# Graph attention and mean aggregation on one core: 45 far chunks with 8 walk blocks each in place of 55 with 6, found rows sent off by ScalarE, smaller opening products, four table buffers

## The chip, the core and the metric

The kernel runs on one core of one Trainium2 chip. A core has five engines that run their own instruction streams in order and wait for one another by semaphores: TensorE (PE, with its weight loads PEld), VectorE (DVE), ScalarE (ACT), GpSimd (POOL) and SyncE (SP). SyncE only issues DMA transfers here; ScalarE and GpSimd issue some too. The metric is the device time of one execution in microseconds (us), and the kernels are compared by the median over runs.

## The reference

There are N = 12,500 nodes with 64 features and E = 400,000 edges sorted by destination; each edge has one of 32 relation types. A first layer computes attention over the incoming edges of each node, a second takes a mean over neighbours:

```python
h_proj = jnp.einsum('nd,rde->rne', h, relation_weight)
t_r = h_proj[etype, src]
h_r = h_proj[etype, dst]
att = jnp.sum(t_r * jnp.tanh(h_r + efeat), axis=-1)
att_exp = jnp.exp(att - segment_max(att, dst)[dst])
a = att_exp / segment_sum(att_exp, dst)[dst]
h_nb = segment_sum(h[src] * a[:, None], dst)
out = leaky_relu((h + h_nb) @ res_w1.T) + leaky_relu(h * h_nb @ res_w2.T)
# x = layernorm(x + out); then x = layernorm(x + mean over in-neighbours of x / out_degree)
```

## The kernel before

The program first writes a table in HBM: for every pair (relation, node) the projected row (64 numbers), together with the node's own row. That is the table stage. Then it goes through the edges in 125 chunks, each of 25 edges on each of 128 partitions. Every edge needs two rows of the table: one for its source (`gs`) and one for its destination (`gd`). After that come short stages for the nodes, for the second layer and for the output, which the diff does not touch.

The source rows are fetched by GpSimd with indirect DMAs, 25 per chunk (L1542). For the destination rows there are two ways, and a chunk is far or near by which it uses.

- In a **far chunk** (the first `FAR` = 55) GpSimd fetches the destination rows too: 25 more indirect DMAs (L1546), 50 in all.
- In a **near chunk** (the other 70) the destination rows lie ready in a scratch tensor `proj_d` in HBM and come with one plain DMA (L1506).

`proj_d` is filled during the far chunks. Since the edges are sorted by destination, the destination rows of the near chunks lie close together in the table, and a "walk" over windows of the table finds them. The walk has `BLOCKS = PER * FAR` blocks of `K` = 15 steps each, `PER` = 6 blocks within each far chunk. A block works as follows:

- SyncE loads the step keys (`keyb`, L1474, 4 slots `KSLOTS`) and 15 windows of the table (`win`, L1470, `WSLOTS` = 3 slots); the first window's number comes out of `sp_tab` by a register load.
- VectorE compares keys with the lane number and writes a 0/1 matrix (`pick`, L1598, `WSLOTS` slots).
- TensorE reads 16 numbers of the block out of `pe_tab` into registers (L1839), opens two accumulation banks with two products of zeros (L1845, 512 columns each), multiplies 15 times `pick` by a window (L1850, at places that the registers give), and adds one carried row (L1852, L1855).
- ScalarE copies the banks to `found` (L1756, two slots) and SyncE sends them to `proj_d` (L1485).

Within a far chunk the code fixes the places of the blocks in each engine's stream: VectorE makes the `pick` of block 0 and 1 ahead of its wait for the chunk's gathered rows (in `front`), of block 2 behind the first sum (L1619), and of 3 to 5 between the steps of the chunk's attention (`back`). ScalarE has its copies (`take_found`) at six places of `chunk`. TensorE does 25 products for a histogram (L1834, it needs the chunk's one-hot matrices `hi`/`lo` of VectorE, L1585) and then the six blocks. A slot of `win` or `pick` is taken again when the block `WSLOTS` back is done (`found_mm`); block b's zeros wait until ScalarE has copied block b-2. GpSimd may start on a chunk when VectorE has written its indices two chunks earlier (`slot_ready`). The near chunks start when all of `proj_d` is written (`found_out`). L1619 in a far chunk and L1624 in a near chunk are the sum of destination row and edge features, the first step of a chunk's attention.

Of the kernel before, what the change touches and what calls it, by code (L numbers as in the profile page):

```python
# [34 lines left out]
FAR = 55  # L35
# [5 lines left out]
PER = 6  # L41
BLOCKS = PER * FAR
UC = -(-(BLOCKS * K + 1) // P)
KSLOTS, WSLOTS = 4, 3
# [789 lines left out]
def gnn_program(nc, x, src, dst, edge_attr, etype, rel_w, res_w1, res_w2, out):  # L834

    ctx = ExitStack()
    with ctx:
# [547 lines left out]
        with ExitStack() as c2:  # L1385
# [22 lines left out]
            rowbuf = sb(c2, "rowbuf", [P, 2, G, RW])  # L1408
# [4 lines left out]
            after = sb(c2, "after", [P, P])  # L1413
            wide = sb(c2, "wide", [P, 2, P])
            group = sb(c2, "group", [P, P])
            work = sb(c2, "work", [P, P])
            steps = sb(c2, "steps", [P, 2, P])
# [4 lines left out]
            pick = sb(c2, "pick", [P, WSLOTS, K * MT])  # L1422
            found = sb(c2, "found", [P, 2, (K + 1) * D])
# [23 lines left out]
            sp_past = sem(c2, "sp_past")  # L1447
# [9 lines left out]
            with nc.Block() as block:  # L1457
                @block.sync
                def _(sp):
# [17 lines left out]
                    def outputs(b, k):  # L1477
                        i0 = nc.values_load(sp_tab[0:1, bass.ds(2 * b + 1, 1)], engines=[mybir.EngineType.SP],
                                            min_val=0, max_val=TILES - 1, skip_runtime_bounds_check_because=MADE)
                        sp.wait_ge(found_ready, b + 1)  # L1480
                        sp.sem_inc(sp_past, 1)
                        if later(b):
                            sp.wait_ge(found_out, 16 * b)
                        sp.sem_inc(sp_past, 1)
                        sp.dma_start(proj_d[:, bass.ds(i0, K + 1), :],  # L1485
                                     found[:, k, :].rearrange("p (i d) -> p i d", d=D)).then_inc(found_out, 16)
# [29 lines left out]
                    outputs(BLOCKS - 2, 0)  # L1516
                    outputs(BLOCKS - 1, 1)
# [43 lines left out]
                def _(dve):  # L1561
# [39 lines left out]
                    def front(c, s, i, link, far=False):  # L1601
# [7 lines left out]
                        if far:  # L1609
                            picks(c, s, i, 1)  # L1610

                    def back(c, s, i, link, far=False, t0=0, t1=G, before=G):
# [12 lines left out]
                        if far:  # L1625
                            picks(c, s, i, 2)
# [10 lines left out]
                        if far:  # L1637
                            picks(c, s, i, 3)
# [14 lines left out]
                        if far:  # L1653
                            picks(c, s, i, 4)
# [5 lines left out]
                            weight[:, t0:t1].unsqueeze(2).to_broadcast([P, n, D]), ALU.mult))  # L1660
                        for w0, w1 in ((0, WH), (WH, W)):
# [8 lines left out]
                        if far:  # L1670
                            picks(c, s, i, 5)
# [79 lines left out]
                def _(act):  # L1751
                    def take_found(b, k):
                        act.wait_ge(found_mm, b + 1)
                        if later(b) and later(b - 1):
                            act.wait_ge(found_out, 16 * (b - 1))
                        nc.scalar.copy(found[:, k, :], acc[k]).then_inc(found_ready, 1)  # L1756

# [5 lines left out]
                    def chunk(c, s, i, far=False, t0=0, t1=G, follows=None):  # L1763
# [3 lines left out]
                        if far:  # L1767
                            if later(c):
                                take_found(PER * c - 1, 1)
                            take_found(PER * c, 0)  # L1770
                        if t0:
# [8 lines left out]
                        if far:  # L1780
                            take_found(PER * c + 1, 1)
# [8 lines left out]
                        if far:  # L1790
                            take_found(PER * c + 2, 0)
# [3 lines left out]
                        if later(i):  # L1795
                            act.wait_ge(stored[s], 16 * i)
                        nc.scalar.copy(rowbuf[:, s, t0:t1, 0:W], run_t[:, :, 1:].rearrange("p w t -> p t w"))  # L1797
                        nc.scalar.copy(rowbuf[:, s, t0:t1, W], mx[:, 1 + t0:1 + t1]).then_inc(rows_ready, 1)
                        act.wait_ge(rows_ready, k + 1)
                        act.dma_start(sums0_v[:, bass.ds(c * G + t0, n), :], rowbuf[:, s, t0:t1, :]).then_inc(stored[s], 16)  # L1800
                        if far:
                            take_found(PER * c + 3, 1)
                            take_found(PER * c + 4, 0)
# [7 lines left out]
                    take_found(BLOCKS - 1, 1)  # L1811
# [14 lines left out]
                def _(pe):  # L1826
# [10 lines left out]
                    def walk(c, j):  # L1837
# [6 lines left out]
                        for h in range(2):  # L1844
                            nc.tensor.matmul(acc[k][:, h * BANK:(h + 1) * BANK], zero[:, 0:P], zero[:, :], start=True, stop=False)  # L1845
# [11 lines left out]

                    histogram(0)
# [52 lines left out]
```

## Time and profile before

| | |
|---|---|
| median of 3 runs | 8621.35 us (8617.23 to 8623.51) |
| the profiled execution | 8620.08 us, of it 8617.3 us from first to last instruction |
| busy: TensorE products, weight loads | 59%, 54% |
| busy: VectorE, ScalarE, GpSimd | 72%, 38%, 67% |
| DMA | 1142.51 MB, 133 GB/s over the span |

The profile is one execution. "Busy" counts the time in which an engine works on an instruction; register loads and DMA issues on TensorE's, SyncE's and ScalarE's sequencers are not counted. A stage has its own limit, so the shares are to be read by stage: the table stage lasts to 452 us, the far chunks about from there to 4014 us, a handover to 4067 us, the near chunks to 6225 us, and the rest to the end.

### The profile page before, as it was taken

What the parts mean: (1) busy time and instruction counts of PE and PEld (TensorE: products, weight loads), DVE (VectorE), ACT (ScalarE), POOL (GpSimd) and SP (SyncE); (2) the same over time, 40 slices, a digit from 0 to 9 for tenths busy, and PEclk for the clock granted to TensorE, in tenths of its full rate; (3) what the DMA queues carried; (4) which work ended last, traced back from release to release, by engine and by line L of the source; (5) the groups of instructions that cost most, each with busy time, mean ns of one, the idle gap of its engine ahead of it and who ended that gap; (6) DMA issues with size and microseconds to landing.
All of it is one profiled execution on the core that took longest, in us unless ns stands there. A gap on an engine that the chain in (4) does not pass through costs nothing. (4 is left out here: it accounts for less than half of the span.)

```text
span 8617.3 us, 133753 instructions
## 1 busy us (share of the span) xinstructions
PE 5065.6 (59%) x44411; PEld 4657.1 (54%) x44577; DVE 6245.6 (72%) x5544; ACT 3266.4 (38%) x4027; POOL 5800.4 (67%) x5165
## 2 busy tenths in 40 slices
PE   6657777777777777776000000000058999999995
PEld 2247676666676667675000000000048888888885
DVE  4546556556555655656887777777779999999996
ACT  3312222212222212212222222222247888888883
POOL 3767777777777777777777777777644555555544
PEclk8855555555555555555555555555559999999996
DMA  9978878877877878787544444444320000000001
GB/s 391 381 176 183 183 178 181 183 177 180 184 178 177 185 176 179 181 180 174 139 129 132 127 133 133 133 133 133 108 52 10 11 10 10 11 10 10 10 11 32
DMA packets 1216482, 1142.51 MB, mean 133 GB/s; under 512 B 993596, under 2 KB 1047422, under 8 KB 1203200
## 3 DMA queue, kind: packets, MB, share of 16 engines
q1 hardware_dynamic: 1036607, 754.44, 34.5%
q0 software_dynamic: 160592, 281.30, 15.0%
q10 hardware_dynamic: 19200, 105.87, 3.1%
q8 instruction: 26, 0.43, 0.0%
q14 instruction: 57, 0.47, 0.0%
HBM read 697.83 MB, written 444.96 MB: 133 GB/s over the span
## 5 line engine op out<-in xcount | busy, mean ns | idle before, releaser
L1542 POOL DMA_INDIRECT gs<-table,idx_s x3125 | 3009.3, 963 | 980.9 <-issue 965.1
L1850 PEld LDWEIGHTS banks<-win,pick 128*125 128x125 f32 x9900 | 2151.1, 332 | 343.9 <-issue 318.3
L1850 PE MATMUL banks<-win,pick 128*125 (+1 forms) x9900 | 2121.0, 413 | 193.2 <-DVE pick L1598 191.7
L764 ACT CAST columns<-ps_u 128x784 bf16<-128x784 f32 x1968 | 1577.3, 812 | 385.7 <-PE ps_u L794 326.7
L647 POOL DMA_INDIRECT tile_row<-tile_rows,now x123 | 1010.5, 8216 | 977.5 <-PE ps_k L784 922.5
L1546 POOL DMA_INDIRECT gd<-table,idx_d x1375 | 1363.0, 991 | 419.1 <-issue 419.1
L1834 PE MATMUL banks<-hi,lo 128*128 128x98 bf16 x3125 | 279.1, 283 | 2002.4 <-DVE hi L1585 2002.4
L1834 PEld LDWEIGHTS banks<-hi,lo 128*128 128x128 bf16 x3125 | 264.1, 146 | 2017.2 <-DVE hi L1585 2017.2
L802 PE MATMUL ps_s<-parts,columns 128*128 128x192 bf16 x12054 | 1314.8, 248 | 0.4 <-ACT columns L764 0.4
L1619 DVE TENSOR_TENSOR gd<-gd,ef 128x1600 f32<-128x1600 f32 x55 | 100.5, 1827 | 1504.1 <-DMA gd<-table,idx_d 1504.1
L794 PE MATMUL ps_u<-yf,hot_l 125*128 125x98 bf16 x15744 | 1054.1, 210 | 159.5 <-DVE yf L711 155.3
L711 DVE TENSOR_TENSOR hot_l<-iota_two,keys_t 125x8192 bf16<-125x8192 bf16 x246 | 1086.9, 4418 | 0.2 <-PE ps_u L794 0.2
L802 PEld LDWEIGHTS ps_s<-parts,columns 128*128 128x128 bf16 x12054 | 1054.0, 140 | 0.6 <-ACT columns L764 0.6
L794 PEld LDWEIGHTS ps_u<-yf,hot_l 125*128 125x128 bf16 x15744 | 878.6, 98 | 222.6 <-DVE yf L711 190.9
L1756 ACT COPY found<-banks 128x1024 f32<-128x1024 f32 x330 | 332.7, 1008 | 1454.6 <-PE banks L1855 1417.0
L711 DVE TENSOR_TENSOR yf<-iota_two,keys_t 125x6272 bf16<-125x6272 bf16 x246 | 840.7, 3417 | 0.0
L1845 PE MATMUL banks<-zero 128*128 128x512 bf16 x495 | 274.6, 624 | 777.4 <-issue 776.5
L1797 ACT COPY rowbuf<-run 128x1625 f32<-128x1625 f32 (+1 forms) x126 | 411.9, 3269 | 778.6 <-DVE run L1662 778.6
L1598 DVE TENSOR_TENSOR pick<-keyb,banks 128x1875 f32<-128x1875 uint8 x330 | 694.5, 2105 | 14.2 <-DMA keyb<-step_keys 1.0
L1777 ACT COPY prod<-gs 128x1600 f32<-128x1600 f32 (+1 forms) x126 | 190.8, 1514 | 976.9 <-DMA gs<-table,idx_s 975.1
L1662 DVE TENSOR_TENSOR_SCAN run<-banks,add 128x858 f32<-128x858 f32 (+1 forms) x252 | 465.9, 1891 | 4.3
L1845 PEld LDWEIGHTS banks<-zero 128*128 128x128 bf16 x660 | 43.2, 110 | 773.4 <-issue 773.4
(313 smaller groups left out, 5922.7 us busy)
## 6 DMA issues: line engine op xcount, KB each, us to landing
proj_d<-found SPq DMA_DIRECT2D x330, 512.0 KB
win<-table SPq DMA_DIRECT2D x660, 240.0 KB
table<-rows SPq DMA_DIRECT2D x98, 1536.0 KB, 8.9
sums<-rowbuf ACTq DMA_DIRECT2D x124, 825.0 KB
ef<-in_edge_attr_dram SPq DMA_DIRECT2D x125, 800.0 KB, 4.7
keyb<-step_keys SPq DMA_DIRECT2D x332, 234.4 KB, 5.3
gd<-proj_d SPq DMA_DIRECT2D x70, 800.0 KB, 6.0
gs<-table,idx_s POOLq DMA_INDIRECT x3125, 2.6
```

The costliest lines, as they stand in the source:

```text
L647: pool.indirect_dma_start(out=rows[:, j % 2, :], out_offset=None, in_=tile_rows, in_offset=bass.IndirectOffsetOnAxis(ap=now[:, j:j + 1], a ...
L711: hot = nc.vector.tensor_tensor(to[0:MT, b, :, :, :], iota_two[0:MT, first:first + wide, :].unsqueeze(1).to_broadcast([MT, QU // 2, wide, 2]),
L764: nc.scalar.copy(columns[:, j % 2, i * UU:(i + 1) * UU, :].rearrange("p (b u) h -> p b (u h)", b=UB), ps_u[n % 2][:, :, 0:UU // UB * NB]). ...
L794: last = nc.tensor.matmul(ps_u[i % 2][:, t // (UU // UB), t % (UU // UB) * NB:(t % (UU // UB) + 1) * NB], hot_l[0:MT, b, u // 2, :, u % 2] ...
L802: last = nc.tensor.matmul(ps_s[s][:, 0:3 * D], columns[:, s, :, h], parts[:, h, :, :].rearrange("p a d -> p (a d)"), start=h == 0, stop=h ...
L1542: pool.indirect_dma_start(out=gs[:, s, g, :], out_offset=None, in_=table_vec, in_offset=bass.IndirectOffsetOnAxis(ap=idx_s[:, s, g:g + 1], ...
L1546: pool.indirect_dma_start(out=gd[:, s, g, :], out_offset=None, in_=table_vec, in_offset=bass.IndirectOffsetOnAxis(ap=idx_d[:, s, g:g + 1], ...
L1598: nc.vector.tensor_tensor(pick[:, k, :], keyb[:, at % KSLOTS, :], lane_ps.to_broadcast([P, K * MT]), ALU.is_equal).then_inc(pick_ready, 1)
L1662: last = nc.vector.tensor_tensor_scan(run_t[:, w0:w1, :].rearrange("p w t -> p (w t)"), keep[:, 0:(w1 - w0) * (1 + n)], add_t[:, w0:w1, :] ...
L1797: nc.scalar.copy(rowbuf[:, s, t0:t1, 0:W], run_t[:, :, 1:].rearrange("p w t -> p t w"))
L1834: last = nc.tensor.matmul(hist, lo[:, g, :], hi[:, g, :], start=False, stop=False)
L1850: nc.tensor.matmul(acc[k][0:MT, bass.ds(slots[t] * D, D)], pick[:, w, t * MT:(t + 1) * MT], win[:, w, bass.ds(at_w, 1), :].rearrange("p o ...
```

## The change

- `FAR` goes from 55 to 45 and `PER` from 6 to 8. There are 80 near chunks and 45 far ones; the number of walk blocks goes from 330 to 360 (the ten chunks more that are near need their destination rows found as well). The lists that the table stage makes grow with it (`UC` from 39 to 43 rows of step keys).
- `WSLOTS` goes from 3 to 4, for `win` and for `pick`. To make room, `rowbuf` has one slot instead of two, and some small tiles of later use lie inside `pick`.
- VectorE makes the `pick` of block 2 ahead of its wait for the gathered rows, and those of 3 to 7 later in the chunk, with one new place ahead of the two scans.
- ScalarE, not SyncE, sends `found` to `proj_d`: `take_found` reads the place from `sp_tab` into a register, copies, waits for the copy and for the previous transfer's landing, and issues the DMA. Two copies of the previous chunk's end move into the chunk itself.
- The two products of zeros of a block have 64 columns instead of 512. Four products of 512 columns clear the banks once at the start.

```diff
-FAR = 55
+FAR = 45
-PER = 6
+PER = 8
-KSLOTS, WSLOTS = 4, 3
+KSLOTS, WSLOTS = 4, 4
...
-            rowbuf = sb(c2, "rowbuf", [P, 2, G, RW])
+            rowbuf = sb(c2, "rowbuf", [P, G, RW])
...
-                            if j >= 2 or later(c):
-                                outputs(PER * c + j - 2, j % 2)
...
                         if far:
                             picks(c, s, i, 1)
+                            picks(c, s, i, 2)
...
+                        if far:
+                            picks(c, s, i, 6)
                         for w0, w1 in ((0, WH), (WH, W)):
...
                     def take_found(b, k):
+                        i0 = nc.values_load(sp_tab[0:1, bass.ds(2 * b + 1, 1)], engines=[mybir.EngineType.Activation],
+                                            min_val=0, max_val=TILES - 1, skip_runtime_bounds_check_because=MADE)
                         act.wait_ge(found_mm, b + 1)
                         if later(b) and later(b - 1):
                             act.wait_ge(found_out, 16 * (b - 1))
                         nc.scalar.copy(found[:, k, :], acc[k]).then_inc(found_ready, 1)
+                        act.wait_ge(found_ready, b + 1)
+                        act.sem_inc(act_past, 1)
+                        if later(b):
+                            act.wait_ge(found_out, 16 * b)
+                            act.sem_inc(act_past, 1)
+                        act.dma_start(proj_d[:, bass.ds(i0, K + 1), :],
+                                      found[:, k, :].rearrange("p (i d) -> p i d", d=D)).then_inc(found_out, 16)
...
                         for h in range(2):
-                            nc.tensor.matmul(acc[k][:, h * BANK:(h + 1) * BANK], zero[:, 0:P], zero[:, :], start=True, stop=False)
+                            nc.tensor.matmul(acc[k][:, h * BANK:h * BANK + D], zero[:, 0:P], zero[:, 0:D], start=True, stop=False)
```

On ScalarE, in the far chunks' loop, the stretch from the tanh (L1779, after the change L1773) to the copy of the scans' result. Before:

```order
L1779 ACTIVATE gd<-gd 128x1600
L1753 REGISTER_ALU
L1755 REGISTER_ALU
L1756 COPY found<-banks 128x1024
L1783 ACTIVATE banks<-ex_in 128x25
L1784 ACTIVATE decay<-ex_in 128x25
L1788 COPY banks<-decay 128x33x25
L1753 REGISTER_ALU
L1755 REGISTER_ALU
L1756 COPY found<-banks 128x1024
L1796 REGISTER_ALU
L1797 COPY rowbuf<-run 128x25x65
```

and after the change, from the same tanh to the end of the second block's sending:

```order
L1773 ACTIVATE gd<-gd 128x1600
L1738 ISA
L1738 TENSOR_LOAD sp_tab
L1740 REGISTER_ALU
L1743 COPY found<-banks 128x1024
L1747 REGISTER_ALU
L1749 ISA
L1749 DMA proj_d<-found 128x1024
L1777 ACTIVATE banks<-ex_in 128x25
L1778 ACTIVATE decay<-ex_in 128x25
L1782 COPY banks<-decay 128x33x25
L1738 ISA
```

Each copy is now followed by its DMA issue on the same engine, ahead of the exponentials of the attention.

On VectorE, in the same loop, from the chunk's first `pick` to the second one behind it. Before:

```order
L1598 TENSOR_TENSOR pick<-keyb,banks 128x1875
L1617 ISA
L1618 REGISTER_ALU
L1619 TENSOR_TENSOR gd<-gd,ef 128x1600
L1598 TENSOR_TENSOR pick<-keyb,banks 128x1875
```

and after the change (L1580 is the `pick`, L1602 the sum):

```order
L1580 TENSOR_TENSOR pick<-keyb,banks 128x1875
L1579 REGISTER_ALU
L1580 TENSOR_TENSOR pick<-keyb,banks 128x1875
L1600 ISA
L1601 REGISTER_ALU
L1602 TENSOR_TENSOR gd<-gd,ef 128x1600
L1580 TENSOR_TENSOR pick<-keyb,banks 128x1875
```

One `pick` more stands ahead of the sum that waits for the gathered rows, so three blocks can run during that wait instead of two.

## Rows read from the trace of the kernel before

**Rows 1.** Windows: us; busy of PE, PEld, DVE, ACT, POOL; clock, DMA, GB/s.

```profile
0.00:452.00 452.00, 275.59 (x932) 101.45 (x933) 228.93 (x387) 163.48 (x393) 226.20 (x345) 0.82 0.98 384
...
516.00:4014.00 3498.00, 2578.54 (x12527) 2434.70 (x12690) 2000.68 (x1891) 734.63 (x703) 2674.49 (x2703) 0.50 0.80 180
...
4067.00:6225.00 2158.00, 154.66 (x1730) 139.75 (x1730) 1720.76 (x1897) 619.70 (x557) 1609.17 (x1706) 0.50 0.48 131
```

**Rows 2.** Groups, 2000 to 4000 us: busy, mean ns | idle before.

```profile
L1546 POOL DMA_INDIRECT gd<-table,idx_d x771 | 768.0, 996 | 235.0 <-issue 235.0
L1542 POOL DMA_INDIRECT gs<-table,idx_s x772 | 762.9, 988 | 235.3 <-issue 235.3
L1598 DVE TENSOR_TENSOR pick<-keyb,banks 128x1875 f32<-128x1875 uint8 x186 | 391.5, 2105 | 7.7
```

**Rows 3.** Groups of instructions, near stage, 4400 to 6000 us.

```profile
L1542 POOL DMA_INDIRECT gs<-table,idx_s x1283 | 1210.6, 944 | 391.0 <-issue 390.1 <-DVE idx_s L911 0.9
```

**Rows 4.** The line L1619 by source, whole run.

```profile
L1619 DVE TENSOR_TENSOR gd<-gd,ef x55: 1824/1825/1883, 516.0 to 4013.6; 128x1600 f32<-128x1600 f32 x55
```

**Rows 5.** TensorE weight loads, 1785 to 1864 us: start, length, [idle before].

```profile
1800.59 0.13 PEld L1845 LDWEIGHTS banks<-zero 128*128 128x128 bf16 x2 [0.73 <-issue]
...
1808.86 0.13 PEld L1845 LDWEIGHTS banks<-zero 128*128 128x128 bf16 x2 [0.69 <-issue]
1813.67 6.38 PEld L1850 LDWEIGHTS banks<-win,pick 128*125 128x125 f32 x30 [4.68 <-issue]
...
1821.74 0.13 PEld L1845 LDWEIGHTS banks<-zero 128*128 128x128 bf16 x2 [1.16 <-issue]
...
1844.79 0.13 PEld L1845 LDWEIGHTS banks<-zero 128*128 128x128 bf16 x2 [5.48 <-issue]
...
1858.04 0.13 PEld L1845 LDWEIGHTS banks<-zero 128*128 128x128 bf16 x2 [3.66 <-issue]
```

**Rows 6.** Timeline of TensorE's products, same stretch.

```profile
1807.69 0.67 PE L1855 MATMUL banks<-found,ident 128*128 x2
...
1813.67 6.56 PE L1850 MATMUL banks<-win,pick 128*125 128x64 f32 x30 [3.78 <-DVE pick L1598]
```

**Rows 7.** The table load L1839 by source: whole run, then three stretches.

```profile
L1839 PEldq TENSOR_LOAD <-pe_tab x330: 3783/3944/7333, 459.4 to 4042.4; - x165
...
L1839 PEldq TENSOR_LOAD <-pe_tab x2: 3791/3799/3807, 1796.8 to 1805.0; - x2
...
L1839 PEldq TENSOR_LOAD <-pe_tab x1: 5808/5808/5808, 1838.9 to 1838.9; - x1
...
L1839 PEldq TENSOR_LOAD <-pe_tab x1: 4832/4832/4832, 1853.1 to 1853.1; - x1
```

**Rows 8.** Timeline of SyncE's DMA issues, 1838.5 to 1846 us.

```profile
1839.04 0.36 SPq L1485 DMA_DIRECT2D proj_d<-found  x1
...
1844.46 0.62 SPq L1485 DMA_DIRECT2D proj_d<-found  x1
```

**Rows 9.** Timeline of VectorE, 1800 to 1870 us.

```profile
1813.44 0.19 DVE L1633 COPY add<-run 128x33 f32<-128x33 f32 x1
...
1824.14 0.18 DVE L1652 TENSOR_TENSOR ex_in<-ex_in,mx 128x25 f32<-128x25 f32 x1
...
1840.21 2.70 DVE L1585 TENSOR_TENSOR hi<-banks,digit 128x2450 bf16<-128x2450 f32 x1
```

**Rows 10.** Timeline of all engines, 4053 to 4070 us.

```profile
4056.82 1.01 ACT L1756 COPY found<-banks 128x1024 f32<-128x1024 f32 x1 [12.36 <-PE banks L1855]
...
4067.11 1.83 DVE L1624 TENSOR_TENSOR banks<-banks,gd 128x1600 f32<-128x1600 f32 x1 [20.14 <-DMA gd<-proj_d]
```

**Rows 11.** DMA issues of the page: KB each, us to landing.

```profile
proj_d<-found SPq DMA_DIRECT2D x330, 512.0 KB
win<-table SPq DMA_DIRECT2D x660, 240.0 KB
...
keyb<-step_keys SPq DMA_DIRECT2D x332, 234.4 KB, 5.3
```

More of the change, by code:

```diff
@@ L1412, in gnn_program @@
             zero = sb(c2, "zero", [P, BANK], BF16)
[L1413 to L1417, printed above, removed]
             goes_on = sb(c2, "goes_on", [P, 1])
@@ L1422, in gnn_program @@
             pick = sb(c2, "pick", [P, WSLOTS, K * MT])
+            after, group, work = (pick[:, 0, at * P:(at + 1) * P] for at in range(3))
+            wide, steps = (pick[:, 0, at * P:(at + 2) * P].rearrange("p (k j) -> p k j", k=2) for at in (3, 5))
             found = sb(c2, "found", [P, 2, (K + 1) * D])
@@ L1637, in back @@
                         if far:
-                            picks(c, s, i, 3)
+                            picks(c, s, i, 4)
                         dve.wait_ge(tanh_done, k + 1)
@@ L1653, in back @@
                         if far:
-                            picks(c, s, i, 4)
+                            picks(c, s, i, 5)
                         dve.wait_ge(keep_ready, k + 1)
@@ L1670, in back @@
                         if far:
-                            picks(c, s, i, 5)
+                            picks(c, s, i, 7)
                         if go_on:
@@ L1767, in chunk @@
                         if far:
-                            if later(c):
-                                take_found(PER * c - 1, 1)
                             take_found(PER * c, 0)
+                            take_found(PER * c + 1, 1)
                         if t0:
@@ L1780, in chunk @@
                         if far:
-                            take_found(PER * c + 1, 1)
+                            take_found(PER * c + 2, 0)
                         act.wait_ge(exp_arg, k + 1)
@@ L1790, in chunk @@
                         if far:
-                            take_found(PER * c + 2, 0)
+                            take_found(PER * c + 3, 1)
+                            take_found(PER * c + 4, 0)
                         if follows:
@@ L1794, in chunk @@
                         act.wait_ge(run_ready, k + 1)
[L1795 to L1798, printed above, removed]
+                        if s or later(i):
+                            act.wait_ge(stored[1 - s], 16 * (i + s))
+                        nc.scalar.copy(rowbuf[:, t0:t1, 0:W], run_t[:, :, 1:].rearrange("p w t -> p t w"))
+                        nc.scalar.copy(rowbuf[:, t0:t1, W], mx[:, 1 + t0:1 + t1]).then_inc(rows_ready, 1)
                         act.wait_ge(rows_ready, k + 1)
-                        act.dma_start(sums0_v[:, bass.ds(c * G + t0, n), :], rowbuf[:, s, t0:t1, :]).then_inc(stored[s], 16)
+                        act.dma_start(sums0_v[:, bass.ds(c * G + t0, n), :], rowbuf[:, t0:t1, :]).then_inc(stored[s], 16)
                         if far:
-                            take_found(PER * c + 3, 1)
-                            take_found(PER * c + 4, 0)
+                            take_found(PER * c + 5, 1)
+                            take_found(PER * c + 6, 0)
+                            take_found(PER * c + 7, 1)
                     chunk(0, 0, 0, True)
@@ L1856, in walk @@
                                          start=False, stop=True).then_inc(found_mm, 1)
+                    for k in range(2):
+                        for h in range(2):
+                            nc.tensor.matmul(acc[k][:, h * BANK:(h + 1) * BANK], zero[:, 0:P], zero[:, :], start=True, stop=True)
                     histogram(0)
```

17 lines of the change are left out of this document (2 added, 15 removed).

## Prediction, made before the changed kernel was run

> **What bounds the kernel now.** I read the windows by stage first [rows 1]. In the far stage (516 to 4014 us) GpSimd is busy 2674 of 3498 us, TensorE's products 2579, VectorE 2001, ScalarE 735; DMA moves 180 GB/s at a share of 0.80. No engine reads as full, so the share alone decides nothing. The groups of a stretch inside it do [rows 2]: GpSimd's two kinds of gather are busy 768.0 + 762.9 us and idle 235.0 + 235.3 us, together 2001 of 2000 us, and all of that idle time is "issue": it waits for no one. So GpSimd paces the far stage, and 54 chunks from the first L1619 to the last [rows 4] give (4013.6 - 516.0)/54 = 64.8 us for one. In the near stage the same holds [rows 3]: 1210.6 + 391.0 = 1602 us, nearly all issue, 1283 gathers in 1600 us, so 31.2 us for 25.
>
> Then the runner-up of the far stage, TensorE. Its timeline shows blocks that run back to back [rows 5]: the zeros of one block start at 1800.59, those of the next at 1808.86, a pitch of 8.27 us, and the idle time between them (0.69, 0.73) is "issue" again. What fills the pitch is not the array. The register load of the next block starts at 1796.8 and lasts 3.79 us [rows 7]: it ends at 1800.6, where the zeros start. A block is 3.79 us of load and some 4.48 us of issuing, one after the other on TensorE's sequencer, and the array waits for it. The load is never under 3.78 us, with a median of 3.94 and up to 7.33 [rows 7]. Six such blocks and the histogram fit into 64.8 us with room, because the blocks then wait for a `pick` (3.78 us before 1813.67, [rows 6]) or for the step before.
>
> **The gathers (POOL).** Each chunk that turns from far to near saves 25 gathers: 64.8 - 31.2 = 33.6 us, ten chunks 336 us, if GpSimd still paces both stages. That is the gross gain.
>
> **The eight blocks (TensorE).** From block 0 to block 7 there are seven pitches, 7 x 8.27 = 57.9 us. From the chunk's last block to the next chunk's first the histogram comes in between: 1844.79 to 1858.04 [rows 5], 13.25 us. The loads in those 13.25 us last 4.83 us [rows 7], 1.04 over the free ones. The sum so far is 71.1 us for a chunk, over GpSimd's 64.8. **TensorE's sequencer becomes the bound of the far stage.**
>
> **The small zeros.** Two products of 512 columns stand for some 0.8 us of array time. In a back-to-back block they cover nothing that is on the path: the sequencer sets the pitch with or without them, so I take 0 of 0.8 us there. Only ahead of the histogram, whose 25 products must get into the array's queue before the sequencer goes on to its load, does a block that ends earlier help; I take 0.35 us per chunk (bounds 0 and 0.8). If the queue were no limit at all they would be worth nothing anywhere.
>
> **ScalarE sends the rows.** Each block adds to ScalarE a register load, which I bound by one sixteenth of TensorE's, 0.24 us, from below and by 3.8 us from above (a single register speaks for the low end), and a DMA issue of 0.36 to 0.62 us [rows 8]; two copies of 1.0 us [rows 10] are added to each chunk. Its busy time of 21% leaves room. What matters is its order. TensorE's load for block b+1 begins once the copy of block b-1 is made, so a copy may come 5 us late. With the eight blocks back to back and time counted from block 0's zeros, products end at 7.4 + 8.27 j. Block 1 ends at 15.7; its copy, its issue and the copy of the source rows let VectorE go on at about 19. In today's trace L1633 starts at 1813.44 and the one-hots are done at 1842.91 [rows 9], 29.5 us; with one more `pick` of 2.1 us [rows 2] that gives 51, where TensorE's histogram is due at 62. ScalarE's exponentials wait for L1652, 10.9 us behind L1633 [rows 9], so they are due at about 30, ahead of block 3's copy at 32. So I cost this edit at nothing; its cover is some 4 us on ScalarE and 11 us on VectorE, and if it went, each us late would be a us per chunk. It also moves the output issues in time, which matters next.
>
> **What stretches a load.** The load of 5.81 us at 1838.9 has an output issue at 1839.04 and a second at 1844.46 beside it [rows 7, 8]; the one of 4.83 stands at a chunk's end; those of 3.79 have none. I read some 1.0 us for each output issue that falls into a load. After the change ScalarE issues block b's output about 1.4 us behind its last product, just behind the load's end, except at the histogram, where the load comes later; that one stretch is in the 71.1 already. Bounds: none stretched gives 1.0 us less per chunk; as many as in the trace now (one at the histogram, about one in the block before and two in the last) 3.2 us more.
>
> The Trainium skill ("Runtime: NRT & Kernel Launch", Instruction fetch mechanics) puts a register load at about 200 ns for each register, which would make the load of 16 numbers 3.2 us by estimate and the chunk 4.7 us shorter, about 66.1 us; the row says 3.79, 237 ns each, and the measurement decides. By that rule the sum below would come out near 8347 us.
>
> **Windows, keys, DMA.** A block moves 512.0 + 2 x 240.0 + 234.4 KB [rows 11] = 1.23 MB, two more per chunk 2.45 MB on top of 180 GB/s x 64.8 us = 11.7 MB. At a pitch of 70.8 us that is a share of 0.80 x 14.1/11.7 x 64.8/70.8 = 0.88, below the 0.98 that the table stage holds [rows 1]. With four slots a window is asked for three blocks ahead. I cost it at 0; were the share at its end (0.98), the chunk would be 64 us, still under TensorE's. The single `rowbuf` waits for a transfer issued a chunk before: 0. The table stage gets 4 key gathers more among its other work; some 1 us each at most if nothing hides them by the duration of [rows 3], I take 3 us.
>
> **The sum.** Pitch P = 57.9 + 13.25 - 0.35 = 70.8 us. In chunk 0 TensorE waits for the `pick` of block 3: 516.0 + 1.8 + 2.1 = 519.9. Block 4's zeros come 8.07 us later (1821.74 - 1813.67, [rows 5]), block 7's at 552.8. Forty-four pitches on: 552.8 + 3115.2 = 3668.0. Its last product ends 7.8 us behind the zeros (1808.36 - 1800.59, [rows 5, 6]), 7.4 with small zeros: 3675.4. From there to the first near chunk it takes 4067.11 - 4056.82 = 10.3 us [rows 10]: 3685.7, against 4067.1 now, 381.4 us earlier. Ten near chunks more cost 312 us. GpSimd's start into the near stage is as now (two chunks ahead, then it waits for VectorE). Net -69 us, with the table stage -66; against the profiled 8620.1 this is 8554, and the median of the runs shown is 1.3 us above that execution, so **about 8554 us**. Each us of P is worth 44 us, and the change breaks even at P = 72.3.
>
> **The rivals.**
> - *GpSimd still paces the far stage* (TensorE's pitch doesn't add up as I say, for instance since loads overlap issuing when nothing else waits). Against it: the two blocks back to back, where nothing was waited for. It gives 8620 - 336 + 3 = 8287 us. Chance 0.08.
> - *The stretched loads decide, and it gets slower.* ScalarE's output issues or SyncE's fall into the loads of TensorE, 1.0 us each. Break-even is at 1.5 such stretches per chunk beyond the one counted; with three, P = 73.8 and 8686 us; with all eight loads hit, P = 77.8 and 8862. For it: the median load of 3.94 us lies above the free 3.79 [rows 7], so about half are hit now, and an issue of ScalarE comes only some 0.5 us behind a load's end. Chance 0.22.
> - *The array's clock rises.* It is at 0.50 (1.2 GHz) in the whole far stage [rows 1] though products cover 74% of it. At 2.4 GHz a block's pitch would stay, being the sequencer's, but the 13.25 us at the histogram would lose the wait for the queue, about 2.2 us: P = 68.6, 8457 us. The Trainium skill ("TensorE: Matmul & The Clock Gate", What's actually happening) has a busy array go to 2.4 GHz; the far stage's row speaks against it so far. Chance 0.05.
> - Anything else that ties up VectorE or ScalarE inside the chunk: 0.04.
>
> **The numbers.** The forecast has 0.61. Its own range is 8510 (no load stretched) to 8625. Half of the slower rival's weight lies below 8690, the clock's about at 8460, so the range of 8 in 10 is 8455 to 8690. A difference of under 0.2% (17 us) can't be told from none with this kernel; that band is P from 71.9 to 72.7. Faster: most of the forecast and the two fast rivals, 0.68; same 0.10; slower 0.22.
>
> **What the changed profile would show.** GpSimd idle for VectorE's indices in the far stage, some 6 us per chunk, in place of issue only; VectorE's long wait no longer for the gathered rows but for ScalarE's copy of the source rows; block pitches of 8.27 throughout and 12.9 at the histogram, with loads of 3.79 and one of 4.8 per chunk; the first L1624 near 3686; clock 0.50. Wrong: a far chunk of 65 us, pitches above 8.3 with loads of 4.8 and more, or TensorE waiting for a `pick`, a window or a copy.

## The result, and the profile after

| | before | changed |
|---|---|---|
| median | 8622.43 us (8617.23 to 8624.12, 4 runs) | 8684.35 us (8679.44 to 8689.97, 4 runs) |
| ratio, 95% interval | | 1.0076 [1.0064, 1.0087] |
| profiled execution, its span | 8620.08, 8617.3 us | 8687.49, 8685.7 us |

The changed kernel is 62 us slower. It was forecast 66 us faster, at 8554. The rival with stretched loads gave 8686 us for a chunk of P = 73.8 us; the result lies inside the wide range of 8455 to 8690 only since that range held part of this rival.

First the stages. Windows of the changed kernel, columns as in [rows 1]:

```profile
0.00:452.00 452.00, 273.73 (x933) 100.80 (x934) 230.70 (x381) 163.39 (x394) 234.82 (x349) 0.84 0.99 385
520.00:3732.00 3212.00, 2638.52 (x13257) 2535.50 (x13257) 1812.13 (x1628) 686.58 (x656) 2155.53 (x2213) 0.50 0.75 193
```

GpSimd, busy 76% of the far stage before [rows 1], is now busy 67% of it. Its groups and the waits from 2000 to 3500 us (waits: engine, line, what was waited for; us in total, times, longest) say why; they answer to [rows 2]:

```profile
L1528 POOL DMA_INDIRECT gd<-table,idx_d x507 | 508.4, 1003 | 154.5 <-issue 154.5
L1524 POOL DMA_INDIRECT gs<-table,idx_s x508 | 479.4, 944 | 358.7 <-DVE idx_d L916 210.3 <-issue 148.4
...
ACT found L1743 <- PE banks L1850: 1030.7, 163, 13.2
DVE add L1616 <- ACT prod L1771: 466.5, 20, 23.5
PEld banks L1840 <- issue: 289.5, 163, 4.9
PE banks L1840 <- issue: 259.4, 163, 4.7
POOL gs L1524 <- DVE idx_d L916: 210.3, 21, 10.0
```

Once per chunk GpSimd now waits 10.0 us for VectorE's indices; VectorE waits 23.5 us for ScalarE's copy of the source rows, and ScalarE waits for TensorE's blocks (L1850 is a block's last product). TensorE waits for nobody: in front of its zeros (L1840) stands "issue", its own sequencer. That is the chain of waits that the prediction named, with TensorE's sequencer at its head. In its length it differs. Three lines by source give the positions of the chunks (count; min/median/max ns; first and last start): the far sum L1602, the first near sum L1607, and the histogram's products L1829 in the stretch from 600 to 3800 us.

```profile
L1602 DVE TENSOR_TENSOR gd<-gd,ef x45: 1817/1818/1847, 519.8 to 3732.6; 128x1600 f32<-128x1600 f32 x45
...
L1607 DVE TENSOR_TENSOR banks<-banks,gd x81: 743/1833/1833, 3822.5 to 6292.7; 128x1600 f32<-128x1600 f32 x79, 128x1024 f32<-128x1024 f32 x1, 128x576 f32<-128x576 f32 x1
...
L1829 PE MATMUL banks<-hi,lo x1075: 204/285/288, 642.3 to 3740.5; 128*128 128x98 bf16 x180
```

The 1075 products are 43 histograms of 25, and the last product of one starts 2.1 us behind the first, so 42 chunks take 3740.5 - 642.3 - 2.1 = 3096.1 us: **73.7 us per chunk**, where 70.8 was forecast and GpSimd needed 64.8 before. The near stage starts at 3822.5 instead of 3685.7.

One chunk shows where the 2.9 us lie. TensorE's weight loads of the zeros and of the histogram, to be read as [rows 5]; they are the zeros of blocks 3 to 7, the histogram, and block 0 of the next chunk:

```profile
2447.31 0.13 PEld L1840 LDWEIGHTS banks<-zero 128*128 128x128 bf16 x2 [1.12 <-issue]
...
2455.57 0.13 PEld L1840 LDWEIGHTS banks<-zero 128*128 128x128 bf16 x2 [1.13 <-issue]
...
2463.84 0.13 PEld L1840 LDWEIGHTS banks<-zero 128*128 128x128 bf16 x2 [1.03 <-issue]
...
2473.77 0.13 PEld L1840 LDWEIGHTS banks<-zero 128*128 128x128 bf16 x2 [2.79 <-issue]
...
2482.03 0.13 PEld L1840 LDWEIGHTS banks<-zero 128*128 128x128 bf16 x2 [1.13 <-issue]
...
2488.94 2.24 PEld L1829 LDWEIGHTS banks<-hi,lo 128*128 128x128 bf16 x25
...
2495.86 0.13 PEld L1840 LDWEIGHTS banks<-zero 128*128 128x128 bf16 x2 [4.68 <-issue]
```

The pitches are 8.26, 8.27, **9.93**, 8.26 and, over the histogram, 13.83 us. The table load behind each (L1834, now the line of the load) and what the other engines issued meanwhile:

```profile
L1834 PEldq TENSOR_LOAD <-pe_tab x1: 3788/3788/3788, 2460.0 to 2460.0; - x1
...
L1834 PEldq TENSOR_LOAD <-pe_tab x1: 5447/5447/5447, 2468.3 to 2468.3; - x1
...
L1834 PEldq TENSOR_LOAD <-pe_tab x1: 5822/5822/5822, 2489.9 to 2489.9; - x1
```

```profile
2456.06 0.35 ACTq L1749 DMA_DIRECT2D proj_d<-found  x1
...
2464.43 0.35 ACTq L1749 DMA_DIRECT2D proj_d<-found  x1
...
2468.53 0.34 ACTq L1795 DMA_DIRECT2D sums<-rowbuf  x1
...
2472.60 0.34 ACTq L1749 DMA_DIRECT2D proj_d<-found  x1
...
2490.85 0.34 ACTq L1749 DMA_DIRECT2D proj_d<-found  x1
2491.35 0.35 SPq L1458 DMA_DIRECT2D ef<-in_edge_attr_dram  x1
```

Two loads per chunk are long, not one. The load at the histogram (2489.9) has block 7's output issue (L1749) and the issue of the edge features' load (L1458) in it and lasts 5.82 us, 2.03 over the free 3.79; [rows 7] had 4.83 there. The load of block 6 (2468.3), which was forecast free, lasts 5.45 us, 1.66 over. It begins 0.2 us ahead of the issue of the chunk's sums (L1795). A load of 3.79 would have ended at 2472.1, and block 5's output is issued at 2472.60, half a microsecond later; the load, still running, takes that in as well. Elsewhere this load lasts up to 7.02 us (at 1803.2). Over 42 chunks of the trace the load at the histogram has a mean of 5.77 us and block 6's one of 5.89 us (5.37 to 7.02); those of the other six blocks have means of 3.79 to 3.80. An output issued 3.9 us ahead of a load (2456.06, the load at 2460.0) leaves it at 3.79.

### The profile page after: what moved, and what is told of

It reads as the page before. It is cut to its first block and busy times, and to the rows that moved or that the text cites. A ratio compares the mean times of both kernels' runs of the same rounds, so it can differ in the third digit from the quotient of the medians.

```text
span 8685.7 us, 137557 instructions
## 1 busy us (share of the span) xinstructions
PE 5191.0 (60%) x45632; PEld 4820.9 (56%) x45633; DVE 6316.1 (73%) x5554; ACT 3315.2 (38%) x4068; POOL 5513.1 (63%) x4919
## 5 line engine op out<-in xcount | busy, mean ns | idle before, releaser
L1524 POOL DMA_INDIRECT gs<-table,idx_s x3125 | 2966.2, 949 | 1414.9 <-issue 953.1
L1845 PE MATMUL banks<-win,pick 128*125 (+1 forms) x10800 | 2359.9, 418 | 36.6 <-DVE pick L1580 29.5
L1845 PEld LDWEIGHTS banks<-win,pick 128*125 128x125 f32 x10800 | 2294.6, 330 | 76.8 <-issue 50.6
L1829 PE MATMUL banks<-hi,lo 128*128 128x98 bf16 x3125 | 278.6, 283 | 2290.7 <-DVE hi L1567 2290.7
L1829 PEld LDWEIGHTS banks<-hi,lo 128*128 128x128 bf16 x3125 | 261.6, 145 | 2308.5 <-DVE hi L1567 2308.5
L1528 POOL DMA_INDIRECT gd<-table,idx_d x1125 | 1112.8, 989 | 342.8 <-issue 342.8
L1743 ACT COPY found<-banks 128x1024 f32<-128x1024 f32 x360 | 364.3, 1012 | 2310.3 <-PE banks L1850 2310.3
L1580 DVE TENSOR_TENSOR pick<-keyb,banks 128x1875 f32<-128x1875 uint8 x360 | 758.2, 2106 | 367.3 <-PE banks L1850 346.7
L1616 DVE COPY add<-run 128x33 f32<-128x33 f32 x126 | 26.2, 208 | 1338.1 <-ACT prod L1771 1338.1
L1840 PE MATMUL banks<-zero 128*128 128x64 bf16 x720 | 102.3, 236 | 582.4 <-issue 579.1
L1563 DVE TENSOR_TENSOR lo<-banks,digit 128x3200 bf16<-128x3200 f32 x125 | 436.5, 3492 | 4.3
```

The costliest lines, as they stand in the source:

```text
L1524: pool.indirect_dma_start(out=gs[:, s, g, :], out_offset=None, in_=table_vec, in_offset=bass.IndirectOffsetOnAxis(ap=idx_s[:, s, g:g + 1], ...
L1528: pool.indirect_dma_start(out=gd[:, s, g, :], out_offset=None, in_=table_vec, in_offset=bass.IndirectOffsetOnAxis(ap=idx_d[:, s, g:g + 1], ...
L1563: nc.vector.tensor_tensor(lo[:, :, :], iota_ps[:, 0:P].unsqueeze(1).to_broadcast([P, G, P]), digit[:, 0, :].unsqueeze(2).to_broadcast([P, ...
L1580: nc.vector.tensor_tensor(pick[:, k, :], keyb[:, at % KSLOTS, :], lane_ps.to_broadcast([P, K * MT]), ALU.is_equal).then_inc(pick_ready, 1)
L1829: last = nc.tensor.matmul(hist, lo[:, g, :], hi[:, g, :], start=False, stop=False)
L1845: nc.tensor.matmul(acc[k][0:MT, bass.ds(slots[t] * D, D)], pick[:, w, t * MT:(t + 1) * MT], win[:, w, bass.ds(at_w, 1), :].rearrange("p o ...
```

## The experiments

The theory after the result: TensorE's sequencer paces the far stage, and two table loads per chunk are long because ScalarE's transfers fall into them. The rival: another wait or the DMA sets the 73.7 us, which a shorter load would leave in place. Each expectation states what it weighs. Line numbers are those of the kernel that the rows come from. Each group of runs had the kernel before beside it: median 8631.06 us for the first four, 8621.18 for the next four, 8629.93 for the last three.

### What the load costs: four numbers, fourteen numbers

Both leave out a part of the computation: numbers that aren't read are replaced by others of the block, so rows land in wrong places; the products and their sizes are the same.

```diff
-                        _, slots = ...(pe_tab[0:1, bass.ds(16 * b, 16)], ...)
+                        _, four = ...(pe_tab[0:1, bass.ds(16 * b + 12, 4)], ...)
+                        slots = [four[t % 3] for t in range(K)] + [four[3]]
```

(For fourteen: `bass.ds(16 * b + 2, 14)` and `some[t % 13]`.)

> The changed kernel, but TensorE's table load of a block reads 4 numbers instead of 16, and the 15 places of the products repeat the first three of them (so rows land at wrong places; the products, their sizes and the register arithmetic are the same). Theory S (TensorE's sequencer paces the far stage: 4.48 us of issuing plus 3.79 us of load per block, one after the other): the load falls to 4 x 0.237 = 0.95 us, the sequencer needs 5.4 us, the array's 7.4 us per block is next, 8 x 7.5 + 2.5 = 62.5 us is under GpSimd's 64.8, GpSimd paces the far stage again and the kernel takes about 8290 us. Rival W (the blocks wait for picks, windows or ScalarE's copies, and the load only fills a wait): no change, 8670 to 8690 us.

> As the run with four numbers, but 14 of the 16 numbers are loaded (places of two products repeat others). Theory S: 2 x 0.237 = 0.47 us less per block, 3.8 us per chunk, 45 chunks: 8684 - 170 = about 8515 us, block pitch 7.80 instead of 8.27. Rival W: no change, 8670 to 8690 us. Rival A (the array, not the sequencer, is the next bound right below 8.27 us): a pitch that stops above 8.0, so 8600 or more.

Measured: four numbers 8281.26 us, ratio 0.9592 [0.9573, 0.9611]; fourteen 8463.88 us, ratio 0.9804 [0.9788, 0.9820]. The load by source, with four and with fourteen:

```profile
L1834 PEldq TENSOR_LOAD <-pe_tab x360: 984/1322/4185, 464.9 to 3388.8; - x180
```

```profile
L1834 PEldq TENSOR_LOAD <-pe_tab x360: 3317/3337/5701, 465.4 to 3572.0; - x180
```

With four the chunk falls to GpSimd's pace and the whole gross gain of the near chunks appears. Fourteen numbers take 3.32 us in place of 3.79 and saved 220 us by the medians, some 235 by the ratios, since the kernel before ran 9 us slower beside this group; 170 were expected. Here the edit is not pure: steps whose two places are now the same number need no register operation (30 of them between two loads instead of 32, with four numbers 20), so some issue time went with the load. The zeros of two blocks with fourteen numbers, at a granted clock of 0.50, have a pitch of 7.57 us, 0.70 less than 8.27, of which the load makes 0.47:

```profile
1340.62 0.28 PE L1841 MATMUL banks<-zero 128*128 128x64 bf16 x2 [0.24 <-issue]
1348.19 0.28 PE L1841 MATMUL banks<-zero 128*128 128x64 bf16 x2 [0.26 <-issue]
```

With four numbers the array itself was faster in part. A stretch of that kernel (columns as in [rows 1]), and the products of a block in it and of one behind it:

```profile
1275.50:1287.00 11.50, 11.50 (x109) 11.50 (x107) 0.00 (x0) 2.02 (x2) 8.76 (x10) 0.95 0.85 196
...
1283.37 3.50 PE L1846 MATMUL banks<-win,pick 128*125 128x64 f32 x30
...
1315.06 6.54 PE L1846 MATMUL banks<-win,pick 128*125 128x64 f32 x30
```

Three blocks of this chunk ran back to back at a granted clock of 0.95, nearly always the higher of the two levels, and the other five at 0.50 (1.2 GHz). So the run with four numbers alone can't tell the array from the sequencer. But its blocks at the lower clock also follow each other at 7.0 us (zeros at 1314.94 and 1321.93), and fourteen numbers leave the clock where it was: the array does such a block in 7.0 us (7.4 was expected), and was not what held 8.27. What paces the changed kernel is TensorE's sequencer, and of it the table load.

### What makes block 6's load long: the sums sent later

```diff
+                        if far:
+                            take_found(PER * c + 5, 1)
                         act.wait_ge(rows_ready, k + 1)
                         act.dma_start(sums0_v[...], rowbuf[:, t0:t1, :]).then_inc(stored[s], 16)
                         if far:
-                            take_found(PER * c + 5, 1)
                             take_found(PER * c + 6, 0)
```

> The changed kernel, with ScalarE's transfer of the chunk's sums issued behind the sending of block 5 instead of ahead of it. Theory D (a load of TensorE is stretched by each large transfer of ScalarE or SyncE that is issued while it runs, about 1 us each; the sums' issue stretches the load ahead of block 6 so far that block 5's output falls into it as well): that load goes from 5.6 to 3.8 us, 1.8 us per chunk, so 8684 - 80 = about 8604 us. Rival V (VectorE's one-hots or ScalarE's large copy, which run beside the same load, stretch it): the load stays at 5.4 us or more and the time within 10 us of 8684.

The next kernel also moves SyncE's load of the edge features (L1458) from step 3 to step 4 of the chunk, away from the histogram:

> As the run with the sums late, and SyncE issues the load of the edge features one block later (at block 4, not 3), so that it no longer falls into the load at the histogram. Theory D: that load goes from 5.7 to 4.8 us (block 7's output still falls into it), 0.9 us per chunk more, so about 8604 - 40 = 8565 us. Rival: only the outputs count, the feature load is harmless: no change against the run with the sums late.

Measured: 8647.08 us, ratio 1.0018 [1.0008, 1.0027], and 8636.45 us, ratio 1.0006 [0.9996, 1.0015]. Both are better than the change (the first by 50 us, going by the ratios), and both fall short of what was expected. The loads of blocks 6 and 7, with the sums late:

```profile
L1835 PEldq TENSOR_LOAD <-pe_tab x1: 3793/3793/3793, 2146.9 to 2146.9; - x1
...
L1835 PEldq TENSOR_LOAD <-pe_tab x1: 4628/4628/4628, 2155.2 to 2155.2; - x1
```

and ScalarE's issues around them:

```profile
2151.24 0.34 ACTq L1749 DMA_DIRECT2D proj_d<-found  x1
...
2151.76 0.50 ACTq L1797 DMA_DIRECT2D sums<-rowbuf  x1
...
2159.51 0.34 ACTq L1749 DMA_DIRECT2D proj_d<-found  x1
```

Block 6's load is back at 3.79, so the sums' transfer was what had made it long. But the next load, which begins 3.4 us behind the issue of the sums, is 0.84 us longer (1.05 by the mean of 42 chunks), and it too has the next output in it (2159.51). That was not foreseen: a transfer of 825 KB issued well ahead of a load can, it seems, still start the stretching. So block 6's load gave 2.1 us per chunk back and block 7's took half of it. Moving the feature load gave 11 us: the load at the histogram goes from a mean of 5.72 to 5.50 us.

### Whether ScalarE's sending is the cause

The changed kernel with SyncE sending, as before; and the kernel before with ScalarE sending and the small zeros:

```diff
 # changed kernel, SyncE's stream
+                            if j >= 2 or later(c):
+                                outputs(PER * c + j - 2, j % 2)
 # take_found as in the kernel before
```

> The changed kernel, but SyncE sends the found rows as before, between its loads of windows and keys. Theory S with D: SyncE issues the outputs two blocks behind in its order, when the windows' slot comes free, right after a block's end and mostly behind TensorE's load; if so the loads stay as they are and the time is within 60 us of 8684. Rival B (ScalarE's sending is what made the change slow): back by most of what was lost, under 8620 us. A third way, that SyncE's stream gets too late with eight blocks: over 8750 us with TensorE waiting for windows or for copies.

> The kernel before (55 far chunks, 6 blocks, 3 slots, both sums buffers), with ScalarE sending the found rows and the small products of zeros. Theory S: GpSimd paces the far stage, TensorE has 64.8 us for six blocks, so neither edit is on the path: within 15 us of 8621. Rival B (ScalarE's sending costs time by itself): slower by 20 us or more.

Measured: 8710.82 us, ratio 1.0107 [1.0090, 1.0124], and 8629.91 us, ratio 1.0009 [0.9999, 1.0019]. With SyncE sending, the load at the histogram and block 6's, in one chunk:

```profile
L1839 PEldq TENSOR_LOAD <-pe_tab x1: 4812/4812/4812, 2201.3 to 2201.3; - x1
...
L1839 PEldq TENSOR_LOAD <-pe_tab x1: 7220/7220/7220, 2177.9 to 2177.9; - x1
```

The first is that of the kernel before again (4.83, [rows 7]), so the second microsecond there comes with ScalarE's sending; some 0.2 us of it is the feature load (the run above), which does not fall into this load when SyncE sends. It is no loss in sum: block 6's load is longer than with ScalarE, at 7.22. There the sums are issued 0.6 us ahead of the load, and SyncE's output falls into it. ScalarE's sending is worth some 26 us here (8710.82 to 8684.35, with medians of before of 8621 and 8622); six blocks don't show it, since GpSimd paces them.

### The zeros

```diff
-acc[k][:, h * BANK:h * BANK + D], zero[:, 0:P], zero[:, 0:D], ...
+acc[k][:, h * BANK:(h + 1) * BANK], zero[:, 0:P], zero[:, :], ...
```

> The changed kernel with products of zeros of 512 columns as before. Theory S: the sequencer sets the pitch of a block with or without them; only ahead of the histogram a block that ends 0.35 to 0.45 us later holds the sequencer back, 45 x 0.4 = 18 us: about 8700 us, block pitch still 8.27. Rival A (the array is on the path of each block): 8 x 0.45 us per chunk, 8684 + 160 = 8845 us.

Measured 8684.44 us, ratio 1.0075 [1.0058, 1.0092]: no difference. The 0.35 us for the way over the histogram is there: from block 7's zeros over the histogram to the next load's start it is 2482.03 to 2489.9, 7.9 us, with small zeros, and 2180.82 to 2189.1, 8.3 us, with wide ones. But the load, which then starts later against block 7's output, is shorter, 5.63 us in place of 5.82 in these two chunks, and block 6's is 5.53. By the means of 42 chunks the two loads together are 0.47 us shorter with wide zeros (5.68 and 5.51 us in place of 5.77 and 5.89), which makes up for the 0.4 us of path.

```profile
2180.82 0.13 PEld L1840 LDWEIGHTS banks<-zero 128*128 128x128 bf16 x2 [0.69 <-issue]
```

```profile
L1834 PEldq TENSOR_LOAD <-pe_tab x1: 5628/5628/5628, 2189.1 to 2189.1; - x1
...
L1834 PEldq TENSOR_LOAD <-pe_tab x1: 5532/5532/5532, 2167.0 to 2167.0; - x1
```

### Issue or bytes: each output in two transfers

```diff
+for h in range(2):
-    act.dma_start(proj_d[:, bass.ds(i0, K + 1), :], found[:, k, :]...).then_inc(found_out, 16)
+    act.dma_start(proj_d[:, bass.ds(i0 + 8 * h, 8), :], found[:, k, 8 * h * D:8 * (h + 1) * D]...).then_inc(found_out, 16)
```

> Changed kernel, each block's found rows sent by ScalarE in two transfers of half the size (32 KB times 8 each, the same bytes and rows in all). If it is the issuing of a transfer that stretches a register load of TensorE, a second issue right behind the first falls into the two stretched loads of a chunk too: each 0.9 to 1.1 us longer, chunk 75.7 us, 8775 us. If it is the bytes on their way that stretch it, nothing changes: loads 5.8 and 5.9, 8684 us.

Measured 8672.47 us, ratio 1.0049 [1.0033, 1.0064], by the ratios some 23 us faster than the change, where one theory expected 91 us more and the other none. The load at the histogram in one chunk, and the issues in it (x2 is two of them):

```profile
L1835 PEldq TENSOR_LOAD <-pe_tab x1: 5509/5509/5509, 1960.4 to 1960.4; - x1
```

```profile
1961.31 0.95 ACTq L1750 DMA_DIRECT2D proj_d<-found  x2
```

A second issue lengthens nothing; the two loads are a little shorter, with means of 5.59 and 5.66 us. So it is not the number of issues. That it is the bytes on their way fits this and the late sums, and the prediction's "1.0 us for each output issue that falls into a load" was the wrong measure. How the chip makes a register load wait was not isolated.

### A shorter load that computes the same

The table's 16 numbers of 8 bits are read as four 32-bit words; shifts and masks in TensorE's registers take them apart.

```diff
-                        _, slots = ...(pe_tab[0:1, bass.ds(16 * b, 16)], ...)
+                        _, words = ...(pe_tab[:, :].bitcast(I32)[0:1, bass.ds(4 * b, 4)], ...)
+                        # place[t] = 64 * number t
+                        word, by = words[t // 4], 8 * (t % 4) - 6
+                        moved = (word & 0xFF) << -by if by < 0 else (word >> by) & 0x3FC0
```

> The changed kernel, with the table load as four 32-bit words that hold four numbers each, taken apart by shifts and masks on TensorE's sequencer. Theory S: the load falls from 3.79 to 0.95 us, and the taking apart adds up to two register operations of some 0.07 us for each of 16 numbers, 1.1 to 2.2 us, so a block is at 6.5 to 7.7 us of sequencer against 7.4 of array, a chunk at 62 to 65 us, and the kernel between 8285 and 8400 us. Rival W: no change. A way in which S holds and the edit fails: the arithmetic costs more than the load saved, over 8684 us.

> The packed kernel with two SyncE/ScalarE transfers moved as in the runs before: the sums go out behind the sending of block 5, the feature load one block later. The theory in which TensorE's sequencer paces only while the table load is long says that there is nothing left to gain, since a load of 0.33 us leaves GpSimd as the pace of the far stage: far chunk 65 us, 8290 us, within 15 us of the packed kernel. The rival, in which the issues cost TensorE something beside the length of its loads, gives 8260 or less.

> Kernel before (55 far chunks, six blocks, SyncE sends) with the table load of four 32-bit words in place of 16 numbers. GpSimd paces its far stage at 64.8 us per chunk with or without the long load, so the theory gives 8620 us, no change: the shorter load pays only together with the change. If the loads had delayed GpSimd's chunks after all, it is faster by more than 20 us.

| kernel | median us | ratio to before |
|---|---|---|
| changed, packed load | 8289.73 (8289.25 to 8292.29) | 0.9617 [0.9601, 0.9633] |
| the same, sums and features late | 8312.23 (8310.69 to 8313.35) | 0.9632 [0.9619, 0.9645] |
| before, packed load | 8607.88 (8602.61 to 8612.42) | 0.9975 [0.9965, 0.9984] |

The first is 395 us faster than the change and 331 us faster than the kernel before. Its load by source, GpSimd's groups from 2000 to 3200 us, and the first waits there:

```profile
L1834 PEldq TENSOR_LOAD <-pe_tab x360: 327/332/1390, 461.1 to 3408.7; - x180
...
L1528 POOL DMA_INDIRECT gd<-table,idx_d x462 | 463.8, 1004 | 140.8 <-issue 140.8
L1524 POOL DMA_INDIRECT gs<-table,idx_s x462 | 455.9, 987 | 140.8 <-issue 140.8
...
ACT found L1743 <- PE banks L1857: 541.3, 96, 8.1
DVE gd L1602 <- DMA gd<-table,idx_d: 435.9, 19, 24.1
```

The load takes 0.33 us instead of 3.79. GpSimd is back at "issue" alone, 462 + 462 gathers in 1200 us, as dense as in [rows 2], and VectorE waits for the gathered rows. TensorE's products, blocks 0 and 1 of a chunk (form as in [rows 6]):

```profile
2120.54 0.31 PE L1847 MATMUL banks<-zero 128*128 128x64 bf16 x2
2120.66 6.54 PE L1852 MATMUL banks<-win,pick 128*125 128x64 f32 x30
...
2127.53 0.31 PE L1847 MATMUL banks<-zero 128*128 128x64 bf16 x2
2127.77 7.04 PE L1852 MATMUL banks<-win,pick 128*125 128x64 f32 x30
...
2135.14 0.32 PE L1847 MATMUL banks<-zero 128*128 128x64 bf16 x2
```

Both ran at a granted clock of 0.50. Block 0 follows the histogram, at which the sequencer gets ahead, and takes 7.0 us: the array's own time again. In block 1 the same 30 products last 7.04 us instead of 6.54, and the pitch is 7.6 us, as in the later blocks where nothing is waited for. So the array isn't yet the limit of a block: the sequencer now has 60 register operations between two loads instead of 32, and spends 0.33 us on the load and 7.3 on issuing, in place of 3.79 and 4.48. Of 3.46 us saved on a load some 0.65 are left per block. The rest of what TensorE gained per chunk is that the two long loads are gone, since no load of this kernel lasts over 1.39 us, and that the way over the histogram is shorter. In the far stage TensorE is then busy nearly throughout, close behind GpSimd:

```profile
520.00:3370.00 2850.00, 2740.27 (x13378) 2682.81 (x13379) 1800.95 (x1627) 686.94 (x658) 2181.27 (x2196) 0.52 0.93 219
```

Sums and features late make the packed kernel 22 us slower by the medians and 13 by the ratios, since the kernel before ran 9 us slower in that group; its far chunk is 65.2 us against 64.9, which makes about 13. That is within the 15 us that were expected, and nothing was gained. The packed load in the kernel before gave 22 us where none was expected: its near stage starts at 4054.4 us in place of 4067.1 [rows 10], 12.7 of the 22; the rest was not located. So the long load cost a little there too. Its far stage also ran at a granted clock of 0.52 to 0.53, not 0.50, and the two were not told apart. Alone, the change loses 62 us and the packed load gains 22; together they gain 331. Nearly all of it belongs to the pair.

## Why the prediction was wrong

**What bounds the kernel.** Right for before (GpSimd's gathers) and right in what takes over (TensorE's sequencer, of which the load is nearly half): the kernels with fourteen numbers and with the packed load show it. The near chunks' 336 us gross came out whole as soon as the load was short: 8281 and 8290 us, the 8287 of the first rival, which the change as made does not reach.

**The eight blocks (TensorE).** Right. The free pitch is 8.27 as read from two blocks. Over the histogram, without its stretch, the chunk shown has 13.83 - 2.03 = 11.80 us; the forecast had 13.25 - 0.35 - 1.04 = 11.86.

**What stretches a load.** This is the step that failed, in its size: 1.04 us per chunk was counted. Measured, by the means of 42 chunks: 1.98 us at the histogram and 2.10 us at block 6 (1.58 to 3.23), 4.1 us together. The remainder agrees: with the free parts as forecast, 70.8 - 1.04 = 69.8 us, the chunk of 73.7 leaves 3.9 us for them. The text said that the output comes "some 0.5 us behind a load's end" and took this for a margin; it was one only as long as nothing else lengthened the load. The issue of the sums by the same ScalarE, which the prediction did not place against the loads at all, used it up. At the histogram the price was read from a kernel in which SyncE sent, 1.04, and it doubled with ScalarE's sending (the SyncE kernel gives 4.81 us back, 1.02 over). The measure itself, 1.0 us for each output issue inside a load, was wrong too: two halves cost no more than one whole, and the sums lengthen a load that begins 3.4 us behind their issue. The bound of "3.2 us more" did hold it: 2.9 us.

**ScalarE sends the rows.** "At nothing" holds for ScalarE's own time: its register load is 0.28 us by median (the low bound was 0.24), and TensorE doesn't wait for a copy in the chunks shown.

```profile
L1738 ACTq TENSOR_LOAD <-sp_tab x360: 272/278/914, 454.8 to 3805.4; - x180
```

As a whole it is worth about 26 us, a gain that wasn't forecast; its cost is in the stretched load at the histogram, its return in block 6's.

**The small zeros.** 0.35 us was forecast and some 0.4 us of path measured, but 0 us of time (8684.44 against 8684.35), since the two loads got longer.

**Windows, keys, DMA.** At nothing, as forecast: TensorE waits for no window in the stretch shown, and the DMA share is 0.75, where 0.88 was estimated.

**The sum.** 44 pitches of 2.9 us more than forecast are 128 us. The rest of the 136.8 us is at the start: the zeros of chunk 0's last block come at 561.68, not 552.8, 8.9 us late. Of these, 3.8 are the longer table stage (the first far sum at 519.8 instead of 516.0), which the prediction put at 3 us outside this sum; the others come since the first chunk's blocks are not back to back.

```profile
561.68 0.27 PE L1840 MATMUL banks<-zero 128*128 128x64 bf16 x2 [0.85 <-issue]
```

**The rivals.** The slower one was right in mechanism and, at its P = 73.8, in time (8686 against 8684), though by two loads stretched by about two microseconds each, not three more of one microsecond; that the time came so near is in part luck. It had 0.22. Its evidence stood in [rows 7]: a load of 5.81 us with two outputs in it, and a margin of half a microsecond against break-even at 1.5 us. Loads that have to stay free beside nine transfers per chunk from ScalarE, with that margin, were no ground for 0.61. The clock stayed at 0.50 in the changed kernel.

## What to carry to other kernels

When a sequencer paces a stage, time its register loads like any other work: look at the width of what they read, and pack it into words before adding blocks. Count what the unpacking adds to the same sequencer: here it took back most of what each load saved, and it paid since the long loads went too. To tell a sequencer from the array, compare the same products where the sequencer had run ahead (6.54 us here) with those where it hadn't (7.04). When the forecast rests on transfers that miss a short window by a fraction of a microsecond, place every issue of every queue against that window, and ask what happens if one of them widens it. An edit that only loses and one that hardly gains can be worth 4% together: when a gross gain fails to appear, find what newly bounds the stage and shorten that before undoing the edit.

## What the runs showed of the hardware

- A register load's time goes with its count of numbers. The free ones took 3.79 us for sixteen 8-bit numbers, 3.32 for fourteen and 0.98 for four. The Trainium skill ("Runtime: NRT & Kernel Launch", Instruction fetch mechanics) has about 200 ns for a register, of loads that it describes as coming from HBM; these rows, of a table in SBUF, agree roughly, with 237 to 246 ns. For four 32-bit words the rows disagree: 0.33 us, 83 ns each, where that rule would make it 0.8 us by estimate. Here width or alignment counts more than the number of registers; these two were not told apart.
- The Trainium skill ("DMA: Bandwidth & Descriptors", Latency and other measured facts) gives some 600 ns as the least for such a load. ScalarE's load of one number took 0.28 us by median and TensorE's of four words 0.33, so the rows lie below it.
- Such loads get longer when a transfer out of SBUF is issued within them or shortly ahead of them: by 0.8 to 3.4 us in the loads shown. A load into SBUF, of the edge features, added some 0.2 us (5.72 to 5.50 us without it). ScalarE's single one also rises to 0.91 us at most. Two half transfers are no worse than one whole. What in the chip makes them wait is open; in the kernel with four numbers, loads with no such issue in them also lasted up to about 2 us.
- The 30 products of a block (f32, 128x64) took 6.54 us at a granted clock of 0.50 and 3.50 us at 0.95, in one kernel. TensorE busy for 96% of 2850 us (packed) was granted only 0.52.
